# Graph attention, GpSimd's gathers: a wait on TensorE's turned masks in front of a group, in place of a wait for the last group's landing

## The reference

```python
h = (x @ W).reshape(N, H, C)                      # 4 heads of 24 channels
alpha_s = jnp.einsum('nhc,hc->nh', h, a_src)
alpha_d = jnp.einsum('nhc,hc->nh', h, a_dst)
e = jax.nn.leaky_relu(alpha_s[src] + alpha_d[dst], NEG_SLOPE)
m = jax.ops.segment_max(e, dst, num_segments=N)
ex = jnp.exp(e - m[dst])
den = jax.ops.segment_sum(ex, dst, num_segments=N)
alpha = ex / (den[dst] + 1e-16)
out = jax.ops.segment_sum(h[src] * alpha[:, :, None], dst, num_segments=N) + b
x = relu(out)
```

## Time and profile before

| | us |
|---|---|
| median of 3 runs | 10468.85 (10465.6 to 10469.36) |
| profiled execution | 10452.31 |
| its span, first to last instruction | 10450.5 |
| message pass, first to last gather | 481.5 to 2796.8 |
| attention passes | from 2982.64, 5472.87 and 7962.01; the last gather of all is at 10298.55 |
| GpSimd busy | 6545.5 (63%) |
| TensorE busy | 6934.4 (66%) |
| granted TensorE clock, mean | 0.601 of full speed |

### The profile page before, as it was taken

How to read it: one execution, slowest core, us unless ns; L and a number is a source line. 1 busy time by engine, 2 the same in 40 slices (tenths; PEclk the granted TensorE clock), 3 DMA queues, 4 the chain that set the end, 5 groups by cost and what they waited for, 6 DMA issues and landing times. The chain is left out here.

```text
span 10450.5 us, 140701 instructions
## 1 busy us (share of the span) xinstructions
PE 6934.4 (66%) x32264; PEld 6106.6 (58%) x32264; DVE 4650.3 (44%) x12446; ACT 3701.4 (35%) x7463; POOL 6545.5 (63%) x6482
## 2 busy tenths in 40 slices
PE   4899999999855555555575555555556555555555
PEld 2288888888745555555565555555556555555555
DVE  5855555555543343434433434343443433443435
ACT  2722222222223333333323333333342333333332
POOL 0166666666446666666636666666664666666662
PEclk8555555555556666666655666666665666566665
DMA  6111111111111111111111111111111111111111
GB/s 119 37 39 39 39 39 39 39 39 39 27 32 36 36 36 36 36 36 36 36 25 36 36 36 36 36 36 36 36 32 29 36 36 36 36 36 36 36 36 25
DMA packets 338291, 393.33 MB, mean 38 GB/s; under 512 B 225462, under 2 KB 232542, under 8 KB 336054
## 3 DMA queue, kind: packets, MB, share of 16 engines
q0 software_dynamic: 206976, 330.75, 15.7%
q1 hardware_dynamic: 131270, 62.12, 3.1%
HBM read 366.44 MB, written 25.99 MB: 38 GB/s over the span
## 5 line engine op out<-in xcount | busy, mean ns | idle before, releaser
L720 POOL DMA_INDIRECT rows<-table_a,idx x4851 | 4881.9, 1006 | 2229.6 <-issue 1453.5
L1258 PE MATMUL ps<-ident,work 128*128 128x128 f32 x4872 | 1214.4, 426 | 2154.9 <-ACT work L1214 2150.5
L1275 PE MATMUL ps<-rows,work 128*128 x9744 | 1865.1, 365 | 822.3 <-ACT work L1207 822.3
L720 POOL DMA_INDIRECT rows<-table_m,idx x1617 | 1611.5, 997 | 1184.8 <-issue 483.8
L1275 PEld LDWEIGHTS ps<-rows,work 128*128 128x128 f32 x9744 | 1731.4, 274 | 1018.0 <-issue 1018.0
L1258 PEld LDWEIGHTS ps<-ident,work 128*128 128x128 f32 x4872 | 939.8, 222 | 2291.9 <-issue 1644.0
L1214 ACT ACTIVATE work<-work,small 128x896 f32<-128x896 f32 x696 | 725.0, 1042 | 3367.9 <-DVE big L1132 3326.2
L1151 DVE SCALAR_TENSOR_TENSOR work<-dstf,big,select 128x224 f32 x696 | 314.1, 451 | 2845.9 <-SPq L666 2845.6
L1140 DVE CUSTOM_DVE_ANT_0 work<-work,ps 128x896 f32<-128x896 f32 x696 | 756.9, 1088 | 1185.9 <-issue 895.2
L1266 PE MATMUL ps<-ident,work 128*128 128x128 f32 x4872 | 1174.3, 418 | 98.3 <-DVE work L1161 98.3
L1266 PEld LDWEIGHTS ps<-ident,work 128*128 128x128 f32 x4872 | 1046.1, 229 | 103.0 <-DVE work L1161 103.0
(11 more groups left out here) (245 smaller groups left out, 7139.2 us busy)
## 6 DMA issues: line engine op xcount, KB each, us to landing
rows<-table_a,idx POOLq DMA_INDIRECT x4851, 2.5
rows<-table_m,idx POOLq DMA_INDIRECT x1617, 2.5
edge_parts<-big SPq DMA_DIRECT2D x6, 1617.0 KB, 7.7
big<-edge_parts SPq DMA_DIRECT2D x231, 42.0 KB
work<-edge_parts SPq DMA_DIRECT2D x50, 192.0 KB
table_a<-work SPq DMA_DIRECT2D x3, 2474.5 KB, 20.6
b_dram<-big SPq DMA_DIRECT2D x3, 1176.0 KB, 8.0
big<-b_dram SPq DMA_DIRECT2D x3, 1176.0 KB, 18.8
```

The source lines that it names most:

```text
L720: pool.indirect_dma_start(rows[:, k % RING, j, 0:width], None, table, bass.IndirectOffsetOnAxis(ap=idx[:, k // CHUNK, at:at + 1], axis=0)) ...
L1258: last = pe.transpose(ps[:, 4 + j // 4, (j % 4) * P:(j % 4 + 1) * P], prob[:, par, j, :], ident[:])
L1275: last = pe.matmul(ps[:, 6 + par, 0:D + 1], probT[:, par, j, :], rows_of(at("slot", 3))[:, j, 0:D + 1], start=(j == 0), stop=(j == TPG - 1))
```

## The change

In the passes without edge features (attention) the wait behind a group's first gather is left out. In front of a group, behind the wait for `freed` and for groups 3 and up, stands a wait until `t_ready` is g-2, which is raised when TensorE has turned the masks of step g-3; the increment of `settled` goes with it. The message pass keeps its order.

```diff
+LEAD = 2
...
                         if not (isinstance(g, int) and g < RING):
                             pool.wait_ge(freed, g - (RING - 1))
+                        if not with_edges and not (isinstance(g, int) and g <= LEAD):
+                            pool.wait_ge(a_sems["t_ready"], g - LEAD)
+                            pool.sem_inc(settled, 1)
                         pool.sem_inc(begun, 1)
                         for j in range(TPG):
                             at = k % CHUNK * TPG + j
                             pool.indirect_dma_start(rows[:, k % RING, j, 0:width], None, table,
                                                     bass.IndirectOffsetOnAxis(ap=idx[:, k // CHUNK, at:at + 1], axis=0)).then_inc(s_gat[k % RING], 16)
-                            if j == 0 and not (isinstance(g, int) and g == 0):
+                            if with_edges and j == 0 and not (isinstance(g, int) and g == 0):
                                 settle((k - 1) % RING, 2 * c + (k - 1) // RING, TPG)
```

## The result

The changed kernel takes 9546.08 us (median of 4 runs, 9543.73 to 9550.95) where the kernel before takes 10467.72 (median of 4 beside it, 10465.6 to 10469.36). The ratio is 0.912, with a 95% interval of 0.9104 to 0.9136. That is 922 us less; 9700 was forecast, with a range from 9630. Its profiled execution took 9545.87 us, its span 9544.0, so 906.5 us less than the span before.

What follows compares the result with a forecast made beforehand. GpSimd's gathers, held by landing waits, were taken as the bound. An attention pass falls from 2335.6 to 2082 us; three save 760, giving 9709, with part of a further 48 us 9700. Range 9630 to 9950.

Steps and rivals of the forecast that it cites:

- The bound: Attention passes: the compute side waits for rows that GpSimd gathers, at 10.12 us a group against 8.75 without waits.
- The landing wait, 488 us: Before attention's second gathers: 675.4 us of idle time less 624 ordinary gaps of 0.30 is removed, 488 us.
- The collisions, 296 less 21 us: Second and third attention gathers held by two-input SBUF VectorE instructions: 296 us goes, 21 us stays, on the fourth gather.
- The long gaps, 22 x (2.82 - 0.30) = 55.4 us a pass: Before the second gather of every tenth attention group: gaps go by the number of gathers and stay, 55.4 us a pass.
- The added wait, nothing: In front of each attention group: wait on TensorE's count hides under the gather before, 0 us; at most 207 us.
- 26 - 15.7 = about 10: Added wait's slack: masks turned 15.7 us after group g-3 starts, three periods are 26 us at least, 10 us of slack.
- Collisions (1): Third gather's need falls inside L1161: period 10.05 us, gain about 50 us, 10420; in half the groups 10065. Both kinds 11%.
- The second kind: VectorE's two-input instructions wait for a gather under way: period 9.81 us, gain 214 us, 10255. Both kinds together 11%.
- Compute pace (2): TensorE's or ScalarE's list loads or the lower clock bring a step to 9.2 to 9.6 us: 9800 to 10100. 8%.
- The gap (3): Added instructions in front of each attention group show in the gap: 0.1 to 0.3 us x 690, 9770 to 9910. 4%.
- The name of the wait (4): `t_ready` is late instead of the landing, so the kernel is slower: at 10.5 us a step, 10730. 3%.
- No effect (5): Something else holds the second attention gather for its 1.03 us: 10469 within 0.2%. 2%.

Runs made afterwards that it cites:

- shift2: Changed kernel plus one 0.8 us-planned VectorE memset (0.70 us) in front of L1155: 9817.28 us, 0.9388; the same memset behind `mask`: 9532.53 us.
- experiment 5: Changed kernel plus needless VectorE memsets in front of L1155, or behind `mask` as controls: 9588.86 against 9530.8 us (two memsets), 9817.28 against 9532.53 (one longer).
- nowait: Kernel before with the attention landing wait left out and no wait on `t_ready` added: 9526.63 us, 0.9115.
- late1: Kernel before with the attention landing wait moved behind a group's second gather, no wait on `t_ready`: 9522.22 us, 0.9117.
- late3: Kernel before with the attention landing wait moved behind a group's fourth gather, no wait on `t_ready`: 9526.15 us, 0.9117.
- lead1: Changed kernel with LEAD 1 in place of 2, so group g waits for step g-2: 9524.56 us, 0.9113.
- extra: Kernel before with one more gather at the start of each attention pass and a wait for it in front of group 1: 10452.34 us, 1.0003.
- front0: Kernel before with the attention landing wait moved in front of a group's first gather, no wait on `t_ready`: 11273.38 us, 1.078.
- lead0: Changed kernel with LEAD 0 in place of 2, so group g waits for step g-1: 14907.25 us, 1.4261.
- both: Kernel before with the wait on `t_ready` added and the attention landing wait kept: 10448.14 us, 0.9999.
- msg3: Changed kernel with the message pass's landing wait moved behind a group's fourth gather: 9474.76 us, 0.9059.
- shift: Changed kernel plus two VectorE memsets, together about 0.5 us, in front of L1155: 9588.86 us, 0.9177; the same behind `mask`: 9530.8 us.

## Why the prediction was right, and where it wasn't

**The bound: right.** Compute waited for GpSimd's rows, and the landing wait set GpSimd's period. Without it, with no other edit, the kernel takes 0.9115 of its time.

**The landing wait, 488 us: right.** No gather in attention waits for a landing, and the idle time that it ended is gone.

**The collisions, 296 less 21 us: right in the main, and 8 us off in size.** 267 us went. That a large two-input VectorE instruction which began before a gather and still runs 0.12 us after its start holds it, and that the gather ends 0.82 us behind that instruction, is shown by `shift2` against its control: 285 us for work that costs nothing elsewhere. The rule was too wide, since it asks only that the instruction be running at the mark (348 gathers of the kernel after, in experiment 5, were so covered and lost nothing). And it was too narrow: "only a two-input SBUF instruction" costs anything. The forecast put the remaining loss on the fourth gather. It sits on the third (mean 0.995 us, the others 0.943 to 0.946), and what holds that one is L1162, which has a single input in SBUF. In four stretches of 90 us (from 3300, 4100, 6400 and 8800) 28 gathers took 0.97 to 1.07 us, and all 28 ended 0.81 to 0.82 us behind an L1162. Over all three passes 537 gathers were held by L1162, 32 us in all, and 12 by L1165, 5 us, where 21 us were put down. The forecast never laid its counterpart, L1158, beside the gathers. The box on SWDGE in the same section of the Trainium skill's page that the forecast cites names such a case: a two-port mode of VectorE, which an fp32 copy within SBUF uses, locks GpSimd out as well. The trace agrees with it for this single-input fp32 instruction; in which mode it ran no row says.

**The long gaps, 22 x (2.82 - 0.30) = 55.4 us a pass: wrong, and this is the step that failed.** It said of the long gap "I take it to go by the number of gathers and to stay". It showed in none of the kernels in which GpSimd's queue has a lead there (`nowait`, `late1`, `late3`, `lead1` and the kernel after), and in `extra` the number of gathers was seen not to matter. The three passes kept 0 us of the 166. Give it back to the sum and the forecast is a gain of 763 + 166 = 929 us, against 906.5 to 922 measured. What the runs showed in its place: a pause of about 1.75 us in GpSimd's instruction stream, at the second gather of every tenth group. The stream runs ahead of the gathers, by 10 us and more in the kernel after. In the kernel before the landing wait had used up the lead at exactly that gather. These rows are the landing wait's increment (L710) in GpSimd's queue of the kernel before, in two groups, the later one being group 16:

```profile
L710 POOLq EVENT_SEMAPHORE  x1: 17/17/17, 3131.2 to 3131.2; - x1
...
L710 POOLq EVENT_SEMAPHORE  x1: 17/17/17, 3141.3 to 3141.3; - x1
```

The second gather follows at 3131.97, 0.75 us later, in the one, and at 3143.75, 2.5 us later, in the other: 1.75 us more. In `front0` and `lead0` there was one gather's worth of lead, and 0.95 us of the pause showed; in `late1` there were 4.6 us, and nothing did. That the pause is in the stream at this place, and costs what the lead doesn't cover, is shown. The rows called the gap "issue", which names no releaser, so they didn't say that this time was the gathers' own. The prediction priced it as that, with the distance of 70 gathers as its only reason, and even thought of it growing by 0.73 us.

What makes the pause, and what counts ten groups, is still open. The number of gathers, the loop's start and the landing wait (by `lead0`) are ruled out; it begins at group 16 of each pass with 16 or with 32 groups written out. Nor is it a place in the code, as it would be if instructions were loaded slowly at one: the loop's body is 16 groups long, so every tenth group falls on eight different places of it, and all 22 have the pause.

**The added wait, nothing: right.** `both` gives 0.9999. The wait is met 10.6 us (median) before the group's first gather, where 26 - 15.7 = about 10 was worked out, and `lead0` gives the 15.7 itself.

**Rivals.** Collisions (1): the third gather's need fell inside L1165 in a handful of groups only; that gather loses 0.05 us a group on the mean, nearly all of it behind L1162, and not 1.06. The second kind, with the lock of the Trainium skill's page "SBUF — State Buffer", "SBUF: two separate sides", would have given a period of 9.81 us (9.57 without the long gaps); it is 8.79. In the kernel after L1155 starts at 6402.86, inside the gather of 6402.47 to 6403.41, and takes its 0.45; the trace does not agree with the page here. Compute pace (2): VectorE still waits 1895.8 us for SyncE, so compute keeps up at 8.8 us a group. The gap (3): 0.30, also in front of first gathers. The name of the wait (4): not at LEAD 2, and fully at LEAD 0. No effect (5): the change is 922 us.

## What to carry to other kernels

An engine that only issues transfers is best seen as a stream with a lead over its work. A wait in it costs the time until it is met and a restart (0.75 us here), and it also lays bare every hiccup of the stream behind it. Move such a wait as few instructions back as it takes for it to be met under work already issued: one gather was as good here as leaving it out. Before a gap that is called "issue" is taken as fixed, ask whether a longer lead would hide it.

Where one engine can hold up another, as VectorE does the gathers here, a change of timing moves collisions as well: lay the new starts over the other engine's instructions for each gather, single-input ones within SBUF too (the third gather's 0.05 us here), and expect that gaps which go will bring gathers onto it (in the message pass the fourth and fifth, which took back 157 of the 210 us of idle time that `msg3` removed).

## What was not expected of the hardware

- A VectorE instruction with one fp32 input and output in SBUF (L1162) holds a gather just as large two-input ones do: 537 gathers of the kernel after end 0.79 to 0.85 us behind it.
- GpSimd's queue has passed the added wait of a group 10.2 to 13.0 us before that group's first gather starts, 8 to 10 gathers ahead; without any such wait (`nowait`) it is 15.3 us ahead in the median.
- From a met wait to the next gather it takes 0.75 us, where a gather with a lead follows after a gap of 0.30.
- The pause of 1.75 us at the second gather of every tenth group, from the 17th on, in each attention pass and in the message pass.
- A VectorE instruction of `shift` and `shift2` with the same shape took 0.33 us behind a memset and 0.45 behind a wait. So work put in front of it cost less than its own duration.
- Some two-input VectorE instructions lie over a gather's 0.12 us mark and don't hold it: L1165 where it began at most 0.04 us before the gather (9 cases), the small L1175 in all 339.
